# Cross-attention and expert kernel: row maxima of a head group copied once to SBUF and sent to the stacked queries by four transfers; TensorE's summing and value runs in another order

## What is computed

```python
y_dca = y[:, -DCA:, :]
y_main = y[:, :-DCA, :]
...
q = _ln((x @ Wq + bq).reshape(b, s1, H, HD), qn_w, qn_b)
...
ctx = _attn(qT, k.transpose(0, 2, 1, 3), v.transpose(0, 2, 1, 3))
...
ctx_dca = _attn(qT, k_dca.transpose(0, 2, 1, 3), v_dca.transpose(0, 2, 1, 3))
...
ctx = ctx + DCA_WEIGHT * ctx_dca
return ctx @ Wo + bo
```

## Time and profile before

| | us |
|---|---|
| median of 3 runs | 995.12 (993.21 to 996.1) |
| the profiled execution | 995.3 |
| its span | 993.6 |
| TensorE busy (matmul) | 909.5 (92%) |
| VectorE busy | 636.0 (64%) |
| ScalarE busy | 459.5 (46%) |
| GpSimd busy | 563.9 (57%) |
| `exps`, L1089 | 138.9, 256 of 595 ns |
| `maxima`, L1136 | 133.9, 60 of 2231 ns |
| `max_row`, L1078, 64 instructions | 0.588 each (median) |

### The profile page before, as it was taken

The page is one execution under the profiler, slowest core; times in us unless marked ns, Lnnn a source line. Parts: engine busy times, 40 slices in busy tenths (PEclk is TensorE's granted clock), DMA queues, the critical chain, the costliest instruction groups (busy, mean ns, idle before and its releaser), DMA issues. The chain is left out here.

```text
span 993.6 us, 16827 instructions
## 1 busy us (share of the span) xinstructions
PE 909.5 (92%) x5047; PEld 406.6 (41%) x5048; DVE 636.0 (64%) x1019; ACT 459.5 (46%) x846; POOL 563.9 (57%) x487
## 2 busy tenths in 40 slices
PE   3889895799999999989999689999999999999898
PEld 1345442122221222246644245555555555555443
DVE  7888777588787988467776144554554444443388
ACT  3375665678877888722353022332233233323540
POOL 5465556367777775543127499989999920000372
PEclk9798998599999999999999799999999999999999
DMA  7234635445454532133425766666566643335676
GB/s 233 77 92 122 179 105 166 139 158 169 167 177 159 177 105 70 53 107 128 153 112 218 289 191 209 217 200 220 201 215 205 201 139 106 121 109 187 232 203 221
DMA packets 106059, 162.26 MB, mean 163 GB/s; under 512 B 12536, under 2 KB 55608, under 8 KB 105616
## 3 DMA queue, kind: packets, MB, share of 16 engines
q1 hardware_dynamic: 92768, 115.86, 35.9%
q0 software_dynamic: 12896, 45.10, 13.6%
q10 hardware_dynamic: 336, 0.57, 0.2%
HBM read 107.88 MB, written 53.48 MB: 162 GB/s over the span
## 5 line engine op out<-in xcount | busy, mean ns | idle before, releaser
L1089 ACT ACTIVATE p_t<-a_psT 128x512 f32<-128x512 f32 x256 | 138.9, 595 | 47.4 <-PE a_psT L1212 46.1
L1136 DVE TENSOR_REDUCE nm<-quad 128x4 bf16<-128x1984 f32 x60 | 133.9, 2231 | 35.7 <-PE quad L1197 35.7
L1905 ACT ACTIVATE e_xT<-quad 128x512 f16<-128x512 f32 x38 | 22.7, 597 | 229.9 <-PE quad L1969 229.9
L1979 PE MATMUL quad<-w_exp,e_xT 128*128 x456 | 107.2, 386 | 4.9 <-DVE e_xT L1933 2.6
L1039 POOL TENSOR_TENSOR p_sum<-p_t,p_t 128x512 f32<-128x512 f32 x64 | 81.1, 1275 | 53.2 <-ACT p_t L1089 53.0
L1979 PE MATMUL quad<-w_exp,e_uT 128*128 x456 | 104.6, 379 | 0.0
L1979 PE MATMUL e_psY<-w_exp,e_gT 128*128 x456 | 104.6, 379 | 0.0
L1212 PE MATMUL a_psT<-q_stk,k_stk 98*128 98x512 f16 x256 | 84.6, 401 | 11.2 <-ACT p_t L1089 9.4
L215 POOL TENSOR_TENSOR w_exp<-e_raw,w_exp 128x1024 f16<-128x1024 f32 x42 | 91.7, 2184 | 3.5
L1936 DVE SCALAR_TENSOR_TENSOR e_g<-quad,bias 128x512 f32<-128x512 f32 x38 | 26.3, 691 | 85.4 <-PE e_psGT L1969 80.5
L1936 DVE SCALAR_TENSOR_TENSOR e_u<-quad,bias 128x512 f32<-128x512 f32 x38 | 26.3, 691 | 73.9 <-PE quad L1979 73.9
(11 more groups left out here) (338 smaller groups left out, 1797.0 us busy)
## 6 DMA issues: line engine op xcount, KB each, us to landing
xs_dram<-zero SPq DMA_DIRECT2D x38, 256.0 KB, 6.9
bias<-in_L_ffn_bup_dram SPq DMA_DIRECT2D x38, 256.0 KB, 3.3
bias<-in_L_ffn_bgate_dram SPq DMA_DIRECT2D x38, 256.0 KB, 3.4
ys_dram<-e_y SPq DMA_DIRECT2D x38, 256.0 KB, 2.0
e_x<-xs_dram SPq DMA_DIRECT2D x36, 256.0 KB, 2.8
q_dram<-q_st SPq DMA_DIRECT2D x24, 256.0 KB, 3.0
k_dram<-k_st SPq DMA_DIRECT2D x24, 256.0 KB, 3.6
q_stk<-q_dram SPq DMA_DIRECT2D x64, 96.0 KB
```

What stands on the lines that cost most here:

```text
L1089: act.activation(probs(w, k), psT[:, k % 2], ACT.Exp, scale=SCALE / (QS * QS)).then_inc(s["exp"], 1)
L1136: dve.tensor_reduce(nm[:, i, :, 0:1].rearrange("p h o -> p (h o)"), psS[:, :, 0:NMAIN], AX.X, ALU.max, negate=True)
L1979: ins = pe.matmul(dst[:, :], stationary, moving, start=(k == 0), stop=(k == len(terms) - 1))
```

## The change

`max_row` goes. In its place ScalarE's `max_copy` copies the whole bank (128 x 512) once for each group into a new SBUF tile `m_row`. The SP queue waits for it at the group's last head (u % 4 == 3), behind that head's stack loads, and issues four transfers of two rows of 1 KB each, from `m_row` to rows 96 and 97 of the four slots. The first used-score pair of a group waits until all four have landed (`row_put`), and the next `max_copy` waits for them too. `sums` waits for the copy instead of for the fourth head's `max_row`. Apart from that, the runs of four are put elsewhere between the pairs.

```diff
+    m_row = sb("m_row", [P, S], F16)
...
+                if u % G == G - 1:
+                    sp.wait_ge(s["mrow"], copied(u // G))
+                    for h in range(G):
+                        sp.dma_start(q_stk[K3:KR, h, :], m_row[h * HD:h * HD + 2, :]).then_inc(row_put, 16)
                 if 0 <= n < NBLK:
                     sp.dma_start(g_["xs_dram"][n * P:(n + 1) * P, :], zero[:, :]).then_inc(g_["xs_zeroed"], 16)
...
-            def max_row(n):
-
-                act.wait_ge(s["m_mm"], n // G + 1)
-                at_least(act, s["t_mm"], TB * (n - SLOTS + 1))
-                act.activation(q_stk[K3:KR, n % SLOTS, :], psX[n % G * HD:n % G * HD + 2, :], ACT.Copy, scale=1.0 / QS).then_inc(s["mrow"], 1)
+            def max_copy(gr):
+
+                act.wait_ge(s["m_mm"], gr + 1)
+                at_least(act, row_put, rows_of(gr - 1))
+                act.activation(m_row[:, :], psX[:, :], ACT.Copy, scale=1.0 / QS).then_inc(s["mrow"], 1)
...
                 if scored(p - 1):
-                    for h in range(G):
-                        max_row(G * (p - 1) + h)
+                    max_copy(p - 1)
...
                 if k == 0:
                     pe.wait_ge(loaded[w % SLOTS], 32 * (w // SLOTS + 1))
-                    pe.wait_ge(s["mrow"], w + 1)
+                    at_least(pe, row_put, rows_of(w // G))
...
             def sums(gr):
-                pe.wait_ge(s["mrow"], min(G * (gr + 2), N))
+                pe.wait_ge(s["mrow"], copied(min(gr + 1, NG - 1)))
...
+                turned_pair(now, 0, 0)
                 if scored(old):
                     sums(old)
-                turned_pair(now, 0, 0)
+                turned_pair(now, 0, 1)
                 if scored(old):
                     third_sums(old)
```

More of the change, by code:

```diff
@@ L976, in attend @@
     raw_ld = sem("a_raw_loaded")
+    row_put = sem("a_row_put")
     zeroed = sem("a_zeroed")
@@ L988, in scored, with copied, rows_of @@
             return 0 <= p < NG
+        def copied(gr):
+            return gr + 1
+        def rows_of(gr):
+            return 16 * G * (gr + 1)
         def probs(n, k):
@@ L1268, in _ @@
                     scores(new, 2)
-                turned_pair(now, 0, 1)
+                turned_pair(now, 1, 0)
                 if scored(old):
                     last_sums(old)
-                turned_pair(now, 1, 0)
+                turned_pair(now, 1, 1)
                 if scored(old):
@@ L1276, in _ @@
                     scores(new, 3)
-                turned_pair(now, 1, 1)
+                turned_pair(now, 2, 0)
                 if scored(old):
                     dca(old)
-                turned_pair(now, 2, 0)
+                turned_pair(now, 2, 1)
                 if scored(old):
                     values(old, 3)
-                turned_pair(now, 2, 1)
                 turned_pair(now, 3, 0)
```

## The result

The changed kernel takes 1082.57 us (median of 4, 1081.61 to 1086.09) against 994.16 us for the kernel before on the same chip: a ratio of 1.0887, with an interval of 1.0866 to 1.0908. The forecast was 1066 us, slower, within 1016 to 1100. Direction and mechanism were right; the loss of 88 us was forecast as 70 to 71.

A forecast was written before the change was run, and what follows sets the result against it. TensorE was taken to bound the attention stage. Each period was R + 10.4 + 1.6 us; losses of +4, +24 and +42 gave +70 on 995.3, so 1066 us, range 1016 to 1100.

The forecast's parts named there:

- R: On TensorE, the start of a group's first pair, which the forecast set by the landing of the four transferred rows.
- 1.6: On TensorE, time lost at the lower clock of 1.2 GHz behind the stall: 1.6 us added to each period.
- 10.4 us of work from R to T: On TensorE, from R to the next T: seven pairs, six runs and two score blocks, 10.4 us.
- T: The start of `max_rows` on TensorE, from which times within a period are counted.
- I take R = T + 6.6 without zero blocks: Periods without zero blocks: fourth issue at T + 4.2, landing 1.9 to 2.6 us later; period 18.6 us against 14.63.
- The upper bound from `k_hi`, T + 8.75: Latest R without zero blocks: T + 2.85 plus the 5.9 us that `k_hi`, behind the same kind of loads, takes to land.
- the rule of the Trainium skill: A DMA's engine count is the largest up to 16 dividing both sides' slowest dimension, lowest-numbered first; rows land near T + 8.2.
- the rows queue behind the loads: Rival: rows wait for the stack loads and land at T + 8.75, or T + 10.15 among zero blocks; 1098 us, chance 0.18.
- R = T + 8.0 among them: Periods in which zero blocks are stored: rows land 1.4 us later than without them; period 20.0 us, nine times.
- the first pair cannot start before T + 4.75: VectorE's maxima start at T + 2.0 and move `scores(new, 1)` to T + 4.4, so the group's first pair follows later.
- +4, +24 and +42: Losses in us: first group, six groups without zero blocks, and the nine periods among zero blocks; together +70.
- the prediction's second rival: Rows come early and VectorE decides, R at T + 4.75: 1000 us, or 1024 with the clock lost; chance 0.14.

The follow-up runs named there:

- the run that took it away: The changed kernel with `max_rows` put behind `scores(new, 0)` and the last pair of the old group: 1085.56 us, ratio 1.0930.

## Why the prediction was right, and where it was off

**Right: what the change is about.** The copy on ScalarE was hidden (R is not set by it in either kernel), SP's place behind the last head's loads was decisive, the stall stands at the first pair, 16 times, and is 3.4 to 4.8 us long ("2.5 to 4.5"), and the clock behind it costs 1.58 us in the pair of periods shown ("1.6"; on the mean of the nine it is 2.0). The 10.4 us of work from R to T stand too: 12.79 less 1.58 and the 0.75 of `max_rows` is 10.46.

**Mis-sized: "I take R = T + 6.6 without zero blocks".** It is T + 7.40 to 7.68 behind the zero blocks, 0.95 us later on the mean. Two parts of this term were too small. An issue of two rows takes 0.64 us from start to start and not 0.43: the fourth starts at T + 4.7 instead of 4.2. And the rows land 2.7 to 3.0 us later and not 1.9 to 2.6. The runs showed why: it is 1.7 us where the last head's loads are issued behind the rows and 1.7 us with loads in three DMAs, so the rest is a queue behind these loads. The upper bound from `k_hi`, T + 8.75, was the right kind of row. By the rule of the Trainium skill that the prediction weighed, the rows would land near T + 8.2, and the measured T + 7.55 is nearer to it than my row's T + 6.6. The rival "the rows queue behind the loads" was thus the better description of the mechanism, at a price in between: I gave it 0.18 and put the likeliest case on the rows nearest in size, where nearest in place (behind the same loads) would have counted for more.

**Right by luck: "R = T + 8.0 among them".** The mean is T + 8.16. But it was T + 6.6, 0.95 too low, plus 1.4 for the zero blocks, where the runs show 0.6 (8.16 less 7.55). Two errors nearly cancel.

**Missed: a wait of `max_rows` for `scaled_dca`,** 0.75 us a period. I followed VectorE's chain through the maxima only; the new order also puts `dca` closer to the next `max_rows`, which writes the same bank (it starts 3.13 us ahead of where `max_rows` would stand without the wait, 402.98 to 406.86 less 0.75, against 4.32 us before, 399.09 to 403.41). As a term of the sum it is the largest that was missing. Behind the zero blocks 18.6 us became 20.30 on the mean: 0.95 for R and 0.75 for this wait. Among them 20.0 became 21.37: 0.16 for R, 0.8 for this wait and 0.4 for the clock. But it is not a loss that can be taken back by itself: the run that took it away was no faster.

**Not reached: "the first pair cannot start before T + 4.75"** for VectorE's sake. With the 0.75 us in it, T itself moves, and `scores(new, 1)` waits only until T + 3.6 (0.35 us); the next group's first maxima start at T' + 1.2 and not at "T + 2.0 at the earliest". The run of the order alone shows what that bound is worth: a period of 15.39 us, where the prediction's second rival had 15.15.

**The sum.** Forecast +4, +24 and +42. Measured from T to T: the first group 18.46 us against 15.16 (+3.3); the second 21.24 against 17.22 (+4.0); the nine 192.37 against 137.57 (+54.8). The four periods behind the zero blocks, 81.21 us (488.07 - 406.86) against 58.53 (403.41 - 344.88), give +22.7, and the rest of the stage +2.7: together 87.5. By the terms of the forecast that is +3.3 for +4, +29.4 for +24 and +54.8 for +42. The range held the time all the same, since it reached up to the queueing case. The second T of the stage stands at 193.25 where it stood at 190.09. SP's row there has the expected shape: the stores end at 179.4, and the four transfers behind them take 3.20 us of issues where the forecast had 1.7.

```profile
176.29 3.07 SPq L1015 DMA_DIRECT2D k_dram<-k_st  x3
179.41 3.20 SPq L1035 DMA_DIRECT2D q_stk<-m_row  x4
```

## What to carry to other kernels

In this kernel a small transfer was as late as the loads ahead of it made it: take its landing from a transfer that stands behind the same loads, not from one of its size, and multiply its issue time by its number. A copy that is hidden under another engine's work is worth nothing when removed, and a route by DMA in its place puts the queue's whole order on the critical path. When a load is cut by an outer dimension of three, look how late its neighbours land; three DMAs of 32 rows made this kernel 0.57% faster where the order of the matmuls offered nothing.

## What the runs showed that I had not expected

A DMA of two rows of 1 KB takes 0.59 us to issue, more than one of 128 rows (0.43 for `q_hi`). Loads in one DMA of three parts made 256 KB stores land after 7.2 us; cut in three they landed after 2.2. And an order that costs 0.76 us in each undisturbed period (15.39 against 14.63) made no difference in the total: it replaced what the late loads had cost, and the first two periods became shorter. Last, stalls of nearly the same length did not cost the same: from the pair behind the stall to the next period the same work took 12.73 to 14.12 us in one execution.
